# Unread matrix products around two routings of a two-layer transformer kernel, and a new order of the first layer's shared products

## What is computed

```
x = x + L0_xattn(layernorm(x), ctx, positions)
x = x + L0_ffn(layernorm(x))
x = x + L1_xattn(layernorm(x), ctx)
x = x + L1_ffn(layernorm(x))
```

```
scores = sigmoid(x @ router_weight.T)          # then two experts per token, weights normalised
routed = sum_e relu(x @ w_up[e])**2 * combine[:, e] @ w_down[e]
shared = relu(x @ shared_up)**2 @ shared_down  # 512 wide, four slices of 128
```

## Time and profile before

| what | before |
| --- | --- |
| median of three runs | 766.83 us |
| lowest and highest | 762.58 and 770.76 us |
| the profiled execution, device time | 768.52 us |
| its span, first to last instruction | 766.6 us |
| mean granted clock of the matrix engine | 0.898 |
| busy share of PE, DVE, ACT, POOL | 84%, 56%, 39%, 34% |

### The profile page before, as it was taken

How to read it: one execution, slowest core, us unless ns; L and a number is a source line. 1 busy time by engine, 2 the same in 40 slices (tenths; PEclk the granted TensorE clock), 3 DMA queues, 4 the chain that set the end, 5 groups by cost and what they waited for, 6 DMA issues and landing times. The chain is left out here.

```text
span 766.6 us, 12462 instructions
## 1 busy us (share of the span) xinstructions
PE 646.2 (84%) x4224; PEld 388.7 (51%) x4224; DVE 425.9 (56%) x1130; ACT 297.3 (39%) x552; POOL 259.2 (34%) x403
## 2 busy tenths in 40 slices
PE   1657988887799999999569999599999999999750
PEld 1542444444566666676335556365666555555330
DVE  4668788863330767967687564448982222222116
ACT  1332777785323122423036667342214232232110
POOL 5350011111135323313101333302258677777140
PEclk9895899998599999999779999759999999999875
DMA  3086122100600464553914310099001899999907
GB/s 116 1 277 197 45 64 64 45 2 1 175 0 1 127 182 151 166 179 97 240 32 126 85 45 2 12 276 245 4 12 36 236 290 276 271 269 279 266 32 274
DMA packets 82615, 99.59 MB, mean 130 GB/s; under 512 B 11610, under 2 KB 58049, under 8 KB 82547
## 3 DMA queue, kind: packets, MB, share of 16 engines
q1 hardware_dynamic: 74738, 86.53, 39.9%
q0 software_dynamic: 5600, 8.53, 4.3%
q10 hardware_dynamic: 2208, 3.67, 1.3%
HBM read 82.42 MB, written 21.63 MB: 136 GB/s over the span
## 5 line engine op out<-in xcount | busy, mean ns | idle before, releaser
L769 DVE TENSOR_REDUCE l_mx<-ps 128x2 f32<-128x512 f32 (+2 forms) x256 | 125.9, 550 | 46.7 <-PE ps L629 46.4
L857 ACT ACTIVATE l_prob<-ps 128x1024 f32<-128x1024 f32 x96 | 98.4, 1026 | 27.0 <-PE ps L659 26.8
L629 PE MATMUL ps<-l_ks,l_qs 48*128 48x256 bf16 (+1 forms) x384 | 73.1, 305 | 26.4 <-DMA l_qs<-l_q_stacks 13.2
L1392 DVE SCALAR_TENSOR_TENSOR xs<-ps,comb,xs 128x256 f32<-128x256 f32 x128 | 55.8, 482 | 59.5 <-PE ps L1052 59.4
L674 PE MATMUL ps<-l_prob,v 128*9 128x256 f32 (+1 forms) x768 | 71.4, 395 | 1.1 <-ACT l_prob L857 1.1
L2146 POOL DMA_INDIRECT y_rows<-r_sw,row x53 | 53.4, 1008 | 44.3 <-DVE r_sw L2287 33.6
L2280 DVE TENSOR_TENSOR r_hot<-r_hot,ps 128x352 f32<-128x352 f32 (+1 forms) x35 | 15.1, 432 | 95.1 <-ACT r_hot L2255 95.1
L1141 POOL TENSOR_TENSOR r_ehid<-r_erelu 128x512 f32<-128x512 f32 x32 | 35.5, 1109 | 83.6 <-ACT r_erelu L1245 83.5
L1790 POOL DMA_INDIRECT xg<-x_rows,r_empty x53 | 56.2, 1060 | 19.9 <-issue 10.5
L1052 PE MATMUL ps<-f_w,r_ehid 128*128 128x256 f32 x256 | 60.8, 381 | 0.2
L1041 PE MATMUL ps<-xT,f_w 128*128 128x512 f32 x128 | 60.0, 593 | 0.0
(11 more groups left out here) (278 smaller groups left out, 1110.4 us busy)
## 6 DMA issues: line engine op xcount, KB each, us to landing
ew<-in_L_w SPq DMA_DIRECT2D x18, 704.0 KB, 8.1
ew13b<-in_L_w SPq DMA_DIRECT2D x12, 704.0 KB, 10.9
f_w<-in_L_w SPq DMA_DIRECT2D x32, 256.0 KB, 2.7
ew<-in_L_w SPq DMA_DIRECT2D x18, 384.0 KB, 9.8
ew2b<-in_L_w SPq DMA_DIRECT2D x12, 384.0 KB, 13.9
ew13b<-in_L_w SPq DMA_DIRECT2D x12, 352.0 KB, 13.1
l_k_stacks<-part SPq DMA_DIRECT2D x8, 384.0 KB, 3.3
l_ks<-l_k_stacks SPq DMA_DIRECT2D x32, 96.0 KB, 2.2
```

The source lines that it names most:

```text
L629: ins = nc.tensor.matmul(ps[:, score_bank(n) + k, qt * S:(qt + 1) * S], qs[row:row + R, u % NBUF, col, qt * P:(qt + 1) * P], ks[row:row + ...
L769: ins = nc.vector.reduce_max(mx[:, u % 2, :, s, head], one[:, :, lo:hi], AX_X)
L857: nc.scalar.activation(prob[:, n % PROBS, :, :, :].rearrange("p h k q -> p (h k q)"), ps[:, 2 + 2 * (n % 2):4 + 2 * (n % 2), :].rearrange( ...
L1392: v.scalar_tensor_tensor(m.xs[:, i, :], m.ps[:, 2 + t, 0:D], m.comb[:, i, e:e + 1], m.xs[:, i, :], ALU.mult, ALU.add).then_inc(e_added, 1)
```

## The change

A new helper issues products that nobody reads: the identity matrix times the identity matrix repeated to 256 columns, into bank 2. It is called once in each of the attention loop's last three passes (n >= PAIRS, after `values` and ahead of `token_sums`), three times before the last two tiles' transposes, three times after their projections, five times at the start of the first routing and seven times at the start of the second: nine in each attention, so 30 in all.

In the first routing, the products `hidden(0)` and `hidden(1)` now lie between the transposes and the logits, their relus lie ahead of the sigmoid on ACT, the three small tables are loaded behind the weights of the first two slices, `values(n - 1)` follows `outputs(n)` instead of `values(n)`, and POOL writes the ones columns two at a time behind the squares of the first eight routed units; the wait on v_set is gone.

```diff
+def keep_running(nc, m, bank, count):
+    for _ in range(count):
+        nc.tensor.matmul(m.ps[:, bank, 0:2 * P], m.ident[:], bcast(m.ident[:], 1, 2), start=True, stop=True)
...
                     values((n - LAG + 1) // (CT // 2) - 1)
+                if n >= PAIRS:
+                    keep_running(nc, m, 2, 1)
                 if turn_at(n) is not None:
                     token_sums(turn_at(n))
...
+            keep_running(nc, m, 2, 3)
             for i in (NT - 2, NT - 1):
                 transposed(i)
             for i in (NT - 2, NT - 1):
                 projected(i)
+            keep_running(nc, m, 2, 3)
...
-            sp.dma_start(bias[:], io["L0_ffn_e_bias"].partition_broadcast(P)).then_inc(ld, 16)
-            sp.dma_start(iota[:], io["iota"][0:E0].partition_broadcast(P)).then_inc(ld, 16)
-            sp.dma_start(later[:], io["later"].partition_broadcast(P)).then_inc(ld, 16)
             for e in range(SH0):
+                if e == 2:
+                    sp.dma_start(bias[:], io["L0_ffn_e_bias"].partition_broadcast(P)).then_inc(ld, 16)
...
-            transpose_and_project(nc, pe, m, xn_ready, xt_ps, xt_ready, rw, E0, logit_ps, 6, ld, 64)
...
-            hidden(0)
+            keep_running(nc, m, 2, 5)
+            transpose_and_project(nc, pe, m, xn_ready, xt_ps, xt_ready, rw, E0, logit_ps, 6, ld, 64,
+                                  lambda: (hidden(0), hidden(1)))
             for n in range(2 * SH0):
-                if n + 1 < 2 * SH0:
+                if 1 < n + 1 < 2 * SH0:
                     hidden(n + 1)
                 outputs(n)
-                values(n)
+                if n >= 1:
+                    values(n - 1)
+            values(NT - 1)
...
-            pool.wait_ge(k_small, 3 * 16)
-            for i in range(NT):
+            def masked_columns(i):
+                if i == 0:
+                    pool.wait_ge(k_small, 3 * 16)
                 for a in range(2):
                     col = (a + 1) * (hd + 1) - 1
-                    ins = nc.gpsimd.tensor_copy(m.v1[:, i, :, col], pmask[:, i % 2, a:a + 1].broadcast_to([P, H]))
-            ins.then_inc(v_set, 1)
+                    nc.gpsimd.tensor_copy(m.v1[:, i, :, col], pmask[:, i % 2, a:a + 1].broadcast_to([P, H]))
...
                 nc.gpsimd.tensor_tensor(ehid[:, n % 2, :], erelu[:, n % 2, :], erelu[:, n % 2, :], ALU.mult
                                         ).then_inc(e_hid_done, 1)
+                if n < NT:
+                    masked_columns(n)
...
+            relued(0)
+            relued(1)
             act.wait_ge(logit_ps, 1)
...
-                if n == 0:
-                    act.wait_ge(v_set, 1)
-                else:
-                    copied_values(n - 1)
+                if n >= 2:
+                    copied_values(n - 2)
+            copied_values(NT - 2)
             copy_half(1)
             copied_values(NT - 1)
...
     pe.wait_ge(xt_ready, NT)
+    between()
     pe.wait_ge(loaded, count)
...
+        keep_running(nc, m, 2, 7)
         for i in range(NT):
             pe.wait_ge(xn_ready, i + 1)
```

More of the change, by code:

```diff
@@ L949, in route_and_experts_l0 @@
         hvar, hwork, sq = sb("hvar", [NT, H]), sb("hwork", [4, NT * H]), sb("sq", [2, D])
-        k_ld, k_small, q_ld, kw_ready, ctx_step, ctx_ready, v_set = (sem(n) for n in (
-            "k_ld", "k_small", "q_ld", "kw_ready", "ctx_step", "ctx_ready", "v_set"))
+        k_ld, k_small, q_ld, kw_ready, ctx_step, ctx_ready = (sem(n) for n in (
+            "k_ld", "k_small", "q_ld", "kw_ready", "ctx_step", "ctx_ready"))
         v_ps, v_copied, k_ps, cent, squared, summed = (sem(n) for n in (
@@ L962, in _ @@
             sp.dma_start(rw[:], io["L0_router_T"].rearrange("(c p) n -> p c n", p=P)).then_inc(ld, 16)
-            sp.dma_start(bias[:], io["L0_ffn_e_bias"].partition_broadcast(P)).then_inc(ld, 16)
-            sp.dma_start(iota[:], io["iota"][0:E0].partition_broadcast(P)).then_inc(ld, 16)
-            sp.dma_start(later[:], io["later"].partition_broadcast(P)).then_inc(ld, 16)
             for e in range(SH0):
+                if e == 2:
+                    sp.dma_start(bias[:], io["L0_ffn_e_bias"].partition_broadcast(P)).then_inc(ld, 16)
+                    sp.dma_start(iota[:], io["iota"][0:E0].partition_broadcast(P)).then_inc(ld, 16)
+                    sp.dma_start(later[:], io["later"].partition_broadcast(P)).then_inc(ld, 16)
                 sp.dma_start(sup[:, e, :, :].rearrange("p c n -> p (c n)"), io["L0_w"][E0 + e, :, 0:KD * I0]
@@ L1149, in _, with relued @@
                 transposed_copy(nc, m, i, i % 2, m.xT).then_inc(xt_ready, 1)
+            def relued(n):
+                act.wait_ge(up_ps, n + 1)
+                if n >= 2:
+                    act.wait_ge(hid_done, n - 1)
+                nc.scalar.activation(relu[:, n % 2, :], ps[:, n % 2, :], ACT.Relu).then_inc(relu_done, 1)
+            relued(0)
+            relued(1)
             act.wait_ge(logit_ps, 1)
@@ L1168, in _ @@
             for n in range(2 * SH0):
-                act.wait_ge(up_ps, n + 1)
                 if n >= 2:
-                    act.wait_ge(hid_done, n - 1)
-                nc.scalar.activation(relu[:, n % 2, :], ps[:, n % 2, :], ACT.Relu).then_inc(relu_done, 1)
+                    relued(n)
                 if n == SH0:
                     copy_half(0)
-                if n == 0:
-                    act.wait_ge(v_set, 1)
-                else:
-                    copied_values(n - 1)
+                if n >= 2:
+                    copied_values(n - 2)
+            copied_values(NT - 2)
             copy_half(1)
@@ L1398, in _, with transpose_and_project @@
                 v.bn_stats(m.bn[:, 4 + t, :], m.xs[:, 4 + t, :])
-def transpose_and_project(nc, pe, m, xn_ready, xt_ps, xt_ready, w, n, logit_ps, bank, loaded, count):
+def transpose_and_project(nc, pe, m, xn_ready, xt_ps, xt_ready, w, n, logit_ps, bank, loaded, count,
+                          between):
     for i in range(NT):
```

## The result

The changed kernel took 758.63 us (median of four runs, 753.37 to 759.17), beside 765.12 us for the kernel before over its three earlier runs and one more: a ratio of 0.9896, 95% interval 0.9848 to 0.9944. Run again beside other kernels it took 760.01 us (median of ten) against 765.48, a ratio of 0.991, interval 0.9873 to 0.9947. The ratios of this document are estimates over the single runs of both kernels and differ a little from the quotient of the two medians (0.9915 and 0.9929 here). The forecast was 758.2 of 766.83 us, 0.9887. The profiled execution took 758.11 us, with a span of 756.3 (before 768.52 and 766.6) and a mean granted clock of 0.926 (before 0.898).

A forecast was written before the change was run, and what follows sets the result against it. The prediction took PE, partly at half clock, to bound the first routing. Savings of 1.83 + 4.95 + 1.63 + 0.25 = 8.66 us off the median of 766.83 gave 758.2 us, range 751 to 764.5.

The forecast's parts named there:

- Price of a product: One added float32 product of 256 columns on PE takes 0.43 us at full clock, 0.86 us at half clock.
- End of layer 0's attention: Projections at full clock end PE 2.19 us earlier, three products behind them give back 0.36: net 1.83 us saved.
- First routing: Transposes 1.2, hidden(0) and hidden(1) 2.7, logits 3.4 us saved, less 0.65 at values(7) and 1.7 for the clock: 4.95 us.
- spell behind the logits: First routing: thin logits let the clock fall behind them; one such fall taken, 1.7 us lost (bounds nothing and 3.4).
- End of layer 1's attention: Same tail with the same lengths as layer 0's: 2.19 less 0.36, less 0.2 for a delayed chain: 1.63 us saved.
- Second routing: Logits wait for r_starts, the clock falls there, logits and shared products stay as they are: 0.25 us saved.
- The first: Rival: the clock falls already in the first routing's transposes; 5.4 us saved in all, 761.5 us; chance 0.2.
- The second: Rival: the second routing keeps the clock as well; 14.3 us saved in all, 752.6 us; chance 0.2.
- The third: Rival: the last stage's stream of expert weights sets the end and swallows all gains ahead; 766.8 us; chance 0.07.
- The fourth: Rival: the added products don't hold the clock and run at half speed themselves; 8.1 us lost, 774.9 us; chance 0.05.

The follow-up runs named there:

- all_best: both_best with values(7) behind the first routed hidden product and one unread product instead of three behind each attention's projections; 751.15 us, ratio 0.9794.
- order_only: The changed kernel without any of the 30 unread products; 762.51 us, ratio 0.9973 to the kernel before.
- first_layer_only: The changed kernel without the 16 unread products of layer 1; 759.61 us, ratio 0.9923 to the kernel before.
- first_best: The changed kernel with its logits in two halves around hidden(1) and without layer 1's 16 unread products; 757.34 us, ratio 0.9888.
- changed_again: The changed kernel itself, unedited, run again beside other kernels; 760.01 us, ratio 0.991 to the kernel before.
- split_logits: The changed kernel with hidden(1) between the logits of tiles 0 to 3 and those of tiles 4 to 7; 755.42 us, ratio 0.9863.
- clears_on_sp: The changed kernel with the 57 semaphore clears of layer 1's attention on SP instead of DVE; 756.72 us, ratio 0.9885.
- last_values: The changed kernel with values(7) behind the first routed hidden product and its copy behind the first routed relu on ACT; 758.8 us, ratio 0.9927.
- products_only: The kernel before with the 30 unread products and nothing else; 763.7 us, ratio 0.9981.
- second_held: The changed kernel with four more unread products in the second routing and its logits waiting for their own weights alone; 757.01 us, ratio 0.9888.
- both_best: first_best with layer 1's 16 unread products and four more, clears on SP, second routing's logits waiting for their own weights alone; 754.19 us, ratio 0.9836.

## Why the prediction was right, step by step

**Price of a product.** 0.43 us: 14 records, seven products, take 3.26 us at the second routing's start with the way out of the array, and end ahead of the first transpose at 488.47:

```profile
484.88 3.26 PE L197 MATMUL ps<-ident 128*128 128x256 f32 x14 [1.73 <-PEq L2425]
```

The five and the seven at the two routings fit their holes as forecast, the six ahead of the last transposes of each attention not quite.

**End of layer 0's attention.** Forecast 1.83, measured 1.53 us. The three products behind the projections cost the 0.36 of the sum (8.57 us with three, 8.21 with one in all_best). The six ahead of the transposes, which I had costed at nothing, cost 0.13: POOL's normalising covers most of them and not all. Without products, at full clock, this end takes 8.07 us (order_only), 2.03 less than before where I had 2.19. And the saving is there only when the clock would have fallen, which it need not.

**First routing.** Without the spell behind the logits the forecast was 1.2 + 2.7 + 3.4 - 0.65 = 6.65; measured are 1.10 for the transposes (4.11 us from the first to hidden(0), before 5.21 to the logits), 2.61 for hidden(0) and hidden(1) (3.54 for 6.15), 3.35 for the logits, and 0.63 lost at values(7); the stage as a whole 6.26. The 1.7 us that I took off for a spell behind the logits are not in the changed kernel's execution, and in five of six they are: 45.75 less 44.06 is 1.69. The forecast of 4.95 lies between the 4.57 us that the stage saves with the spell and the 6.26 without. Taken from a row elsewhere, this term was right in its place, its size and its uncertainty, and it pointed at the edit that removes it.

**End of layer 1's attention.** Forecast 1.63, measured -0.13: this step failed. I had written that it is the same tail with the same lengths. The lengths of PE's rows are the same; DVE's 58 clears stand only here, because layer 0 has no old semaphores (the first clear of the whole trace is at 257 us). The kernel's text and the trace both had them, and a releaser named PE, so I did not look. With the clears on SP the end takes 9.85 us, 1.30 less than before. Part of what is missing of the 1.63 is the delay by the six products ahead of the transposes, which I had at 0.2 and which is 0.34 to 0.35 us: the transposes start 5.14 us behind the last values product with these products and 4.80 without, in first_layer_only and first_best.

**Second routing.** Forecast 0.25, measured 2.60 (2.45 to 2.33 in changed_again and split_logits, 0.86 and 0.95 in clears_on_sp and last_values). The step that failed is that the clock would fall ahead of the logits, and logits and shared products would stay as they are. In the changed kernel it falls inside the logits: these take 5.60 us for 6.88, the shared products behind them 3.45 for 4.41. In others it falls inside the logits or just ahead of them, as the execution has it. That the logits then wait for r_starts was right: they begin at 493.25, and the wait ends with the landing at 493.12.

```profile
493.25 5.80 PE L203 MATMUL ps<-r_gw,xT 128*128 128x61 f32 x32 [1.14 <-DMA r_starts<-in_starts]
```

**The rivals.** The first (the clock falls in the first routing's transposes) is refuted: 4.11 us with nothing but transposes on PE, granted 1.00:

```profile
195.29:199.40 4.11, 2.95 (x16) 1.60 (x17) 2.21 (x7) 2.78 (x8) 0.00 (x0) 1.00 0.60 162
```

The rule from which it would follow by the Trainium skill ("TensorE: Matmul & The Clock Gate", "Part 4: PE-mode transpose"), that transposes don't count as PE's other work does, is not what these rows show; products_only, where the clock fell right behind the same transposes, leaves open that they count for less. The second (the second routing holds its clock) came true in part, and in second_held, with four more products and without the wait for r_starts, wholly. The third (the last stage swallows the gain) falls for the kernel as a whole, since the interval of its ratio lies below 1; for the second layer's part both_best speaks against it, and that a part is swallowed stays open. The fourth (the products run at half clock themselves) did not occur.

So the total was right in part by luck, because two misses of opposite sign met: 1.76 us too much at layer 1's end, and 2.35 too little in the second routing, of which the last stage may have taken a part back. The first layer, with 6.8 of the 8.66 us, was right by its own steps (6.1 to 7.8 measured, with and without the spell behind the logits). The time also lies nearer than the gain: 758.63 us against 758.2, but the kernel before came out at 765.12 and not at 766.83, so that by the medians 6.5 us were gained (5.5 in the second set of runs) where 8.66 were forecast.

## What to carry to other kernels

Where a matrix engine's clock falls behind thin work, try the order first: put full, useful products between two thin stretches (transposes, products with few columns), and divide a thin stretch, before adding unread ones. In the first routing here the order alone saved 3.3 us and the unread products alone 0.4, in one profiled execution each; the totals of these two kernels can't be told apart. Unread products pay only in holes that a wait makes anyway, and even there they cost something (0.13 and 0.35 us) where a chain over other engines starts behind one of them. When a wait ends in an engine's row, look at what that engine's own queue issued in it: semaphore clears are not counted as busy, and the releaser that the profile names need not be what decides. Price a stage's gain by several executions read down one column when the clock's spells wander.

## What the runs showed of the hardware that I had not expected

A semaphore clear costs DVE 83 ns in its queue (57 in 4.77 us). On SP the 57 are done by 463 us, 24 us ahead of the next block, and nothing waits for them (clears_on_sp). A stream of 32 float32 weight loads with 16 columns each halves with the clock just as full products do (6.84 to 3.49 us). And the same code keeps or loses the granted clock from one execution to the next: layer 0's end without added products ran at 0.50 in one execution and at 1.00 in another, and the changed kernel, unedited, had no spell behind the first routing's logits in one execution and one of 3.4 us in the other.
